# A list scheduler's cost table, hand-over times and row leads are changed in a four-row interleaved transformer kernel

## The reference

```python
x = x + tanh(g_xattn[l]) * attention_l(layernorm(x), ctx)
x = x + tanh(g_ffn[l])   * feed_forward_l(layernorm(x))
```

## Time and profile before

| | |
|---|---|
| median of 3 runs | 1038.44 us (1036.83 to 1040.66) |
| profiled execution, first to last instruction | 1044.5 us |
| PE busy in it | 876.9 us (84%), 7316 matmuls |
| DVE busy | 790.5 us (76%) |
| ACT busy | 492.8 us (47%) |
| POOL busy | 302.3 us (29%) |
| mean granted TensorE clock | 0.909 |

### The profile page before, as it was taken

One profiled execution on the slowest core, in us unless ns is written; L12 is line 12 of the kernel. 1 busy time (PEld: TensorE's weight loads), 2 busy tenths in 40 slices (PEclk: granted clock), 3 DMA queues, 4 the chain that ended last, 5 costly groups with the idle time before them and its releaser, 6 DMA issues.

```text
span 1044.5 us, 19277 instructions
## 1 busy us (share of the span) xinstructions
PE 876.9 (84%) x7316; PEld 566.3 (54%) x7316; DVE 790.5 (76%) x1849; ACT 492.8 (47%) x753; POOL 302.3 (29%) x324
## 2 busy tenths in 40 slices
PE   4777867878898999987899776878888799999886
PEld 3433336534566678863565323565445575788543
DVE  6799998888774845388668998989786667455983
ACT  3655453356533422327875735433635244322575
POOL 4510245444443201110233013364534332011100
PEclk9999878898898999997999987888989898999899
DMA  9100000000000000000001000000000000000000
GB/s 318 45 3 2 2 1 1 1 3 2 2 1 1 2 1 1 1 7 7 27 27 42 1 3 1 2 1 2 3 3 1 1 2 2 1 1 1 2 8 17
DMA packets 11741, 14.26 MB, mean 14 GB/s; under 512 B 1604, under 2 KB 10716, under 8 KB 11396
## 3 DMA queue, kind: packets, MB, share of 16 engines
q1 hardware_dynamic: 11552, 12.88, 3.8%
q10 hardware_dynamic: 100, 0.14, 0.1%
HBM read 11.55 MB, written 1.05 MB: 12 GB/s over the span
## 4 chain that ended last, share of the span: by engine, by line
PE 45%; DVE 40%; ACT 7%; issue 6%; DMA 1%; POOL 1%; SPq 0%; ACTq 0%; DVEq 0%
PE banks L997 41%; DVE nm_row L1454 12%; DVE probs L1473 5%; PE banks L692 3%; DVE qf_row L1484 2%; ACT probs L953 2%; DVE st_row L1297 1%; DVE xn_row L1409 1%; DVE wide L1543 1%; DVE mv_row L1299 1%; ACT kT_row L870 1%; DVE oh_row L1519 1%; PE banks L1051 1%; DVE qr_row L1439 1%; DVE ix_row L1513 1%
## 5 line engine op out<-in xcount | busy, mean ns | idle before, releaser
L1454 DVE TENSOR_REDUCE nm_row<-banks 128x4 f32<-128x1024 f32 (+1 forms) x192 | 210.2, 1127 | 35.7 <-PE banks L997 35.1
L953 ACT ACTIVATE probs<-banks 128x1024 f32<-128x1024 f32 (+1 forms) x144 | 128.5, 932 | 40.7 <-PE banks L997 40.2
L786 POOL TENSOR_TENSOR rstd_row<-rstd_row,neghalf 128x2 f32<-128x2 f32 x66 | 47.2, 716 | 272.4 <-DVE rstd_row L1404 217.8
L997 PE MATMUL banks<-probs,vpad 128*32 128x256 f32 (+1 forms) x1536 | 110.4, 408 | 12.1 <-ACT probs L948 6.5
L997 PE MATMUL banks<-wide,c 128*128 128x256 f32 x512 | 119.9, 388 | 0.0
L997 PE MATMUL banks<-qT_row,kT_row 50*128 50x256 bf16 (+2 forms) x896 | 90.5, 298 | 28.3 <-DVE nm_row L1454 12.9
L997 PE MATMUL banks<-kT_row,qT_row 48*128 48x256 bf16 (+2 forms) x896 | 94.0, 299 | 17.4 <-DVE nm_row L1454 9.1
L997 PEld LDWEIGHTS banks<-wide,c 128*128 128x128 f32 x512 | 95.5, 192 | 15.7 <-issue 0.7
L948 ACT ACTIVATE probs<-probs 128x1024 f32<-128x1024 f32 x64 | 67.2, 1055 | 63.7 <-DVE probs L1473 62.3
L786 POOL TENSOR_TENSOR kss_row<-kss_row,neghalf 128x32 f32<-128x32 f32 x8 | 44.3, 5532 | 140.5 <-DVE kss_row L676 140.5
L997 PEld LDWEIGHTS banks<-qT_row,kT_row 50*128 50x128 bf16 (+1 forms) x896 | 41.3, 110 | 70.5 <-issue 23.5
(11 more groups left out here) (220 smaller groups left out, 1566.5 us busy)
## 6 DMA issues: line engine op xcount, KB each, us to landing
c<-in_c SPq DMA_DIRECT2D x1, 2500.0 KB
wide<-in_mask SPq DMA_DIRECT2D x8, 256.0 KB, 3.0
qT_row<-mT_row SPq DMA_DIRECT2D x96, 4.0 KB
c<-in_c SPq DMA_DIRECT2D x1, 1194.5 KB
xn_row<-in_ctx SPq DMA_DIRECT2D x8, 128.0 KB, 3.7
x_row<-in_x SPq DMA_DIRECT2D x8, 128.0 KB, 3.1
late<-in_late SPq DMA_DIRECT2D x2, 512.0 KB, 15.4
out<-x_row SPq DMA_DIRECT2D x8, 128.0 KB, 1.9
```

The lines of the kernel that those rows point to most:

```text
L786: return pool.tensor_tensor(t, t, neghalf[:, 0:n], ALU.pow)
L953: act.activation(dst[:, :, 0:w], src[:, :, 0:w], ACT.Exp, scale=1.0 if l == 2 else HD ** -0.5).then_inc(sem["probs"], 1)
L997: return pe.matmul(dst, lhsT, rhs, start=start, stop=stop, **kw)
L1454: V.tensor_reduce(nm[b][:, t, :, 2 * jp:2 * jp + 2], ps[:, :, :, 0:kn], AX.X, ALU.max, negate=True).then_inc(sem["max"], 1)
```

## The change

It changes numbers of the play, and two rules in it. No instruction of any step, no tile and no semaphore is touched; what changes in the program is the order of steps on each engine and the banks and slots that they get.

1. `COST`: nearly every time is replaced. Most PE times become smaller (`max` of layer 3 from 0.5 to 0.22, `attend` from 0.4 to 0.23, `choose` from 0.35 to 0.11), some larger (`q_flip` of layer 2 from 1.7 to 2.09). `deep` on ACT goes from 2.2 to 0.91, `attend` 0 on ACT from 1.13 to 0.95; `norm` gets longer times in four places; `max` 1 on DVE is now 0.6 for its four half-width parts and 1.13 for the others, where it was 0.87 for all.
2. `HOP`: PE's hand-over from 0.32 to 0.21, the others a little less. A step that starts on PE pays `WAKE` = 0.1 on top of the hand-over from another engine.
3. `SWITCH`: `array(s)` names the shape in which a step leaves and finds the TensorE array (whole, halves, strips, sides, low). When the step starts in another shape than the last one left, the play adds 0.1 us before it.
4. `LEAD` is now a table by row and sublayer; in it all eight values of a row are the same. Rows 0 to 3 keep nearly their leads. Of the later four, whose order by lead was 5, 7, 6, 4, the order is now 7, 6, 4, 5.

```diff
-LEAD = [278.1, 297.8, 281.0, 302.6, -18.0, 11.8, -8.3, 1.7]
+LEAD = [[280.1] * 8,
+        [299.3] * 8,
+        [281.4] * 8,
+        [303.3] * 8,
+        [-15.0] * 8,
+        [-24.0] * 8,
+        [-5.7] * 8,
+        [4.9] * 8]
...
-        "q_flip": [("PE", .6), ("ACT", .92)], ("q_flip", 2): [("PE", 1.7), ("ACT", .97)],
-        "max": [("PE", .5), ("DVE", 1.13)], ("max", 0): [("PE", .85), ("DVE", 1.13)], ("max", 1): [("PE", .75), ("DVE", .87)],
-        ("max", 2): [("PE", 1.2), ("DVE", 1.13)],
-        "attend": [("PE", .4), ("ACT", .92)], ("attend", 0): [("PE", .4), ("DVE", 1.13), ("ACT", 1.13)],
-        "weigh": [("PE", 1.03)], ("weigh", 1): [("PE", .82)], ("weigh", 2): [("PE", 1.9)], "divide": [("ACT", .49)],
-        "deep": [("PE", 1.65), ("ACT", 2.2)], "deep_out": [("PE", 3.6), ("DVE", .6)], "store": [("SP", .1)]}
-PLACING = 0.45
+        "q_flip": [("PE", .44), ("ACT", .91)], ("q_flip", 2): [("PE", 2.09), ("ACT", 1.07)],
+        "max": [("PE", .22), ("DVE", 1.13)], ("max", 0): [("PE", .75), ("DVE", 1.13)], ("max", 1): [("PE", .55), ("DVE", 1.13)],
+        ("max", 2): [("PE", .95), ("DVE", 1.13)],
+        "attend": [("PE", .23), ("ACT", .91)], ("attend", 0): [("PE", .23), ("DVE", 1.13), ("ACT", .95)],
+        "weigh": [("PE", .9)], ("weigh", 1): [("PE", .69)], ("weigh", 2): [("PE", 1.76)], "divide": [("ACT", .49)],
+        "deep": [("PE", 1.72), ("ACT", .91)], "deep_out": [("PE", 3.64), ("DVE", .52)], "store": [("SP", .1)]}
+PLACING = 0.43
...
-HOP = {"PE": .32, "DVE": .14, "ACT": .16, "POOL": .12, "SP": .1}
+HOP = {"PE": .21, "DVE": .12, "ACT": .145, "POOL": .09, "SP": .1}
+WAKE, SWITCH = .1, .1
...
+    if s[:2] == ("max", 1) and s[3] < 4:
+        own = [("PE", .44), ("DVE", .6)]
...
+def lag(other, eng):
+
+    o, e = other
+    return HOP[e] + (LANDS.get(o[0], 0) if e == "SP" else 0) + (WAKE if eng == "PE" else 0)
+
+def array(s):
+
+    kind, l = s[:2]
+    if kind == "max" and l < 2:
+        return ("whole", "halves") if l == 0 else ("halves", "whole")
+    if kind in ("max", "attend"):
+        return "halves", "halves"
+    if kind in ("weigh", "shift_flip") or (kind == "choose" and l != 1) or (kind in ("k_flip", "q_flip") and l == 2):
+        return "strips", "strips"
...
+    return "whole", "whole"
...
-            return (-left[s, eng] - LEAD[s[2]], s[2])
+            return (-left[s, eng] - LEAD[s[2]][s[1]], s[2])
...
-                lands = LANDS.get(other[0][0], 0) if other[1] == "SP" else 0
-                t = max(t, ended[other] + HOP[other[1]] + lands)
+                t = max(t, ended[other] + lag(other, eng))
...
-            clear[eng] = ended[s, eng] = end = now + dict(phases(s))[eng]
+            begins = now
+            if eng == "PE":
+                first, last = array(s)
+                if first != mode:
+                    begins = max(now, clear[eng] + SWITCH)
+                mode = last
+            clear[eng] = ended[s, eng] = end = begins + dict(phases(s))[eng]
```

More of the change, by code:

```diff
@@ L173, in phases @@
         own = [(e, us + PLACING) if e == "ACT" else (e, us) for e, us in own]
-    return own
+    if s[:2] == ("max", 1) and s[3] < 4:
+        own = [("PE", .44), ("DVE", .6)]
+    return own
+def lag(other, eng):
[9 more added lines that the diff above has]
+        return "strips", "strips"
+    if kind == "choose":
+        return "strips", "whole"
+    if kind == "o_flip":
+        return "sides", "sides"
+    if kind == "spread":
+        return "low", "low"
+    if (kind in ("expand", "inner") and l == 2) or kind == "fore" or (kind == "outer" and l == 0):
+        return "low", "whole"
+    return "whole", "whole"
 def starts_after(s, eng):
@@ L360, in work_left @@
                 for eng, _ in phases(s):
-                    ahead = [(o, e, HOP[e] + (LANDS.get(o[0], 0) if e == "SP" else 0)) for o, e in starts_after(s, eng)]
+                    ahead = [(o, e, lag((o, e), eng)) for o, e in starts_after(s, eng)]
                     if eng in former:
                         ahead.append((former[eng], eng, 0))
-                    for o, e, lag in ahead:
+                    for o, e, wait in ahead:
                         if o[2] == s[2]:
-                            after.setdefault((o, e), []).append((s, eng, lag))
+                            after.setdefault((o, e), []).append((s, eng, wait))
                     former[eng] = s
@@ L370, in work_left @@
                 for eng, us in reversed(phases(s)):
-                    left[s, eng] = us + max([lag + left[n, e] for n, e, lag in after.get((s, eng), [])], default=0)
+                    left[s, eng] = us + max([wait + left[n, e] for n, e, wait in after.get((s, eng), [])], default=0)
         return left
@@ L396, in place @@
         pending, former = {}, {}
+        mode = "whole"
         rank = {s: b for b, line in enumerate(lines) for s in line}
```

45 lines of the change are left out of this document (23 added, 22 removed).

## The result

| | before | after |
|---|---|---|
| median of the runs on one chip | 1037.63 us (4 runs, 1034.75 to 1040.66) | 1052.68 us (4 runs, 1051.38 to 1053.21) |
| ratio, 95% interval | | 1.0142 [1.0111, 1.0173] |
| profiled execution, first to last instruction | 1044.5 us | 1051.5 us |

The change made the kernel 1.4% slower, and the forecast was 1.1% faster. The span of an execution lies about 1.7 us under its time (1051.5 against 1053.21 here), so the profiled execution of before took about 1046 us and is slower than each of the four runs above. The two profiles therefore show only 7 of the 15 us.

What follows compares the result with a forecast made beforehand. PE and DVE bound the kernel in turns, stage by stage. Span 1044.5 - 8.4 (waits) - 4 (seam) + 1 (table loads) + 0 (clock) = 1033.1 us, so 1027 us measured; forecast range 1010 to 1033, wider range 1009 to 1051.

Steps and rivals of the forecast that it cites:

- The first term, the shortened waits: PE's five largest wait groups, 84.4 us together, shrink by a tenth through better times: 8.4 us saved, range 0 to 28.
- The second term, the seam: Between the two row groups, row 7 goes before row 5 and fills idle DVE time: 4 us saved, at most 9.8.
- The third, table loads at `deep`: On ACT, exponentials put between gelus add table loads: 1 us lost, range 0 to 5.1.
- The fourth, the clock: PE's time at the lower clock may shift with the order: taken as 0, 8 us either way per 40 us.
- A: Rival: same time, as DVE and PE are each full in their stages; 1033.2 to 1043.6 us, chance 0.20.
- C: Rival: larger gain, a third of PE's late-step waits and the whole seam saved; about 1001 us, chance 0.07.
- B: Rival: slower, PE priced at full clock only, so DVE starves at 100-200 and 600-720 us; about 1052 us, chance 0.19.
- D: Rival: slower by clock alone, PE fed less evenly; 1046 us, decided from about 60 us more at 1.2 GHz; chance 0.08.
- its two signs: If the clock moved, its mean is no longer 0.909 and the stages at 100 to 200 us show it.

Runs made afterwards that it cites:

- splices: Three kernels planned with the new numbers, each group of rows made to follow before's or after's order: 1041.29, 1044.48 and 1056.11 us.
- late_leads_back: The kernel after with the old leads for rows 4 to 7 alone: 1058.12 us, ratio 1.0210.
- after_feed_late: The kernel after with two extra 512-column matmuls, results overwritten, in each `attend` step of attention 1: 1047.54 us, ratio 1.0114.
- new_then_old: Rows 0 to 3 in after's order, rows 4 to 7 in before's; interleaving and banks from the new numbers: 1041.29 us, ratio 1.0029.
- after_feed: The kernel after with two extra 512-column matmuls, results overwritten, ahead of each `attend` of attention 0: 1061.39 us, ratio 1.0218.
- before_feed: The kernel before with two extra 512-column matmuls, results overwritten, ahead of each `attend` of attention 0: 1034.55 us, ratio 0.9974.

## Why the prediction was wrong

**The first term, the shortened waits (-8.4 us), is the step that failed.** Its reason held: the new PE times are right at full clock, and the five groups of the earlier trace rows fell by 15.4 us, more than I took. Its tacit premise, that the waits which remain stay what they were, did not. xn_row and stack took 17.5 us more, PE idled as long as before (167.7 and 167.6 us), and the second group got 11 us longer. The splices put that on the second group's own order: it costs 11.4 to 11.6 us, with either order of the first group.

A second premise stands behind it: I took the old order for a typical product of the old numbers, so that better numbers could only tidy it. But the old leads fit the old table (the play ends at 995.0 us, and at 1008.1 with leads 0.3 to 0.5 away), and what they reach on the chip, 1037.6 us, no fitted plan of the new numbers or of their dearer versions reaches (1044.1 to 1052.7). Whether this is luck as well isn't shown: it would take several fitted plans of the old table, and there is one.

**The second term, the seam (-4 us), came out in its size, but not by its mechanism, which is luck.** The first group was through 3.9 us sooner, and row 7's `max` 0 came first. The term held that this would come from row 7 taking row 5's place. In late_leads_back, whose first group has the leads of after and where row 5 goes first as in before, the last store of the first group and the first `max` 0 come just as early:

```profile
550.32 0.59 PE L1033 MATMUL banks<-brief_row,identb 128*128 128x512 bf16 x2
...
551.16 0.41 SPq L796 DMA_DIRECT2D out<-x_row  x1
```

The splices give 3.2 to 3.4 us to the first group's own order. DVE, which was to work over 28 of the 40 us after row 3's store, worked 22.16 from 512.2 to 552.2 us, and 22.97 in before from 514.8 to 554.8.

**The third, table loads at `deep` (+1 us), had the wrong sign.** The page of after has fewer loads over the whole span, 9 against 11: one serves the first pair of gelus (L1030, two in a row), another the second pair.

```profile
506.62 1.28 ACT L1030 ACT_TABLE_LOAD   x1 [0.90 <-PE banks L1040]
507.92 1.94 ACT L1030 ACTIVATE wide<-banks 128x1024 f32<-128x1024 f32 x2
509.87 1.28 ACT L996 ACT_TABLE_LOAD   x1
```

**The fourth, the clock (0, with 8 us either way for 40 us), was mis-sized.** After passes 31 us more at 1.2 GHz. By the term's own rate that is 6 us, and the runs give 5.1 us (after against after_feed_late; 2.9 by the ratios). If the filler costs after what it costs before, 4.2 us, the clock's part is 7 to 9 of the 15; this is an estimate, and that premise isn't shown. What I had missed is that the mean of the clock says little: new_then_old has 0.897 and takes 1041.3 us, after has 0.895 and takes 1052.7. It seems to matter where PE has the chain, as from 700 to 900 us here; where DVE was the bound, from 600 to 700 us, a rise from 0.82 to 0.88 brought nothing. Every run of the table with a ratio under 1.013 has a clock of 0.90 or more in that stretch, and all but one of the slower ones lie below 0.90. That alone could as well be the waits lowering the clock; only the filler in attention 1 speaks for the other direction.

**The rivals.** A and C are out by the time. B named 1052 us, the right number for the wrong reason: DVE's share in its two places stayed at 197.96 of 220 us, 90%, where it had to fall below 85%, and 14 us more of PE work there changed nothing. (27 us more changed nothing in before; after_feed lost 8.7 us by it, behind that stage.) D, slower by the clock alone, is right in part. It held that the places where DVE sets the pace would lose, and asked for 60 us more at the lower clock, where 31 came; of its two signs the mean fell, but 100 to 200 us didn't move down (0.84, before 0.81). Its 13 us for 60 us more are 12 by the rate of the fourth term.

**Two sums of the working.** 703 and 788 us for the new play leave out its rule for the four narrow `max` 1 steps of each row. With it PE's times sum to 699.5 us and DVE's to 770.8: DVE's sum didn't rise towards the measured 790.5 but stayed (773 before), and B's 19 us by which DVE is the busier engine are 6. The forecast doesn't rest on either.

**What stays open.** Which steps of the second group's order make PE's load uneven from 700 on isn't settled; late_leads_back and new_then_old, whose leads put rows 4 to 7 in the same sequence, are already 17 us apart. Nor is the gap of 6 to 8 us that is left when both orders are fed. And no version here beats the kernel before by more than the measurement can tell: the best, before_feed, has 1 inside its interval.

## What to carry to other kernels

When a kernel's order comes from a greedy play on the host, compare a change of its numbers only between plans whose leads were fitted to their own numbers: leads moved by 0.5 us off their fit cost 9 to 16 us here, and the play's own end would have shown most of it before any run. Trust that end within one table, and not between tables: the one with the more exact full-clock prices preferred the order that is slower on the chip. A change of the table has to be followed by a new selection on the chip, over several fitted plans. Where PE has the chain and the granted clock is below 1, try useless matmuls at the start of that stretch: if the time falls, the clock is part of the bound.

## What the runs showed of the hardware

- More work on TensorE can make a kernel faster: 27 us of filler in attention 1 brought the mean clock from 0.895 to 0.919 and the time from 1052.7 to 1047.5 us (2.9 us by the ratios). In before it raised the mean clock from 0.909 to 0.922 and cost 4.2 us. The same filler in attention 0 raised the clock where it stood (0.82 to 0.88 in 600 to 700 us) and helped nothing; after took 1061.4 us with it.
- 256 matmuls more, 14 us of PE work, are free in attention 0 of both kernels: 0.998 [0.9947, 1.0013] for before, and 1.0137 beside the 1.0142 of after.
- A busy share hides the clock: in 800 to 900 us PE is busy 91.11 us with 563 matmuls at a clock of 0.85, and 90.40 us with 691 at 1.00. The two stretches hold not quite the same steps, since the rows stand further on in one; the sum over 700 to 900 is the fairer comparison.
